# Sixteen-head attentions on one core: one tile of keys weighed at a time, and the small products made over two steps

## What is computed

```python
# L1, once: causal, 16 heads of 8 features
qkv = einsum('btc,cd->btd', x, w_qkv) + b_qkv
scores = einsum('bhqd,bhkd->bhqk', q, k) * scale
attn = softmax(where(causal, scores, min), axis=-1)
out = einsum('bhqk,bhkd->bhqd', attn, v)
return einsum('btc,cd->btd', out, w_out) + b_out

# L3, twice: M = 2 attentions of 16 heads each, no mask
q  = einsum('btd,mdhk->mbhtk', n1, mha_wq) + mha_bq
kk = einsum('btd,mdhk->mbhtk', n1, mha_wk) + mha_bk
v  = einsum('btd,mdhk->mbhtk', n1, mha_wv) + mha_bv
attn = softmax(einsum('mbhtk,mbhsk->mbhts', q, kk) / sqrt(KD), axis=-1)
ctx = einsum('mbhts,mbhsk->mbthk', attn, v)
x = x + einsum('mbtd,bm->btd', einsum('mbthk,mhkd->mbtd', ctx, mha_wo) + mha_bo, mha_probs)
```

## Time and profile before

| | |
|---|---|
| median of three runs | 2229.13 us |
| the profiled execution | 2221.16 us, span 2219.4 us |
| TensorE (PE) busy | 1751.5 us, 79% of the span |
| weight loads (PEld) busy | 902.8 us, 41% |
| VectorE (DVE) busy | 1308.6 us, 59% |
| ScalarE (ACT) busy | 1137.3 us, 51% |
| POOL busy | 609.9 us, 27% |
| mean granted clock of TensorE | 0.897 of full speed |

### The profile page before, as it was taken

How to read it: one execution, slowest core, us unless ns; L and a number is a source line. 1 busy time by engine, 2 the same in 40 slices (tenths; PEclk the granted TensorE clock), 3 DMA queues, 4 the chain that set the end, 5 groups by cost and what they waited for, 6 DMA issues and landing times.

```text
span 2219.4 us, 36295 instructions
## 1 busy us (share of the span) xinstructions
PE 1751.5 (79%) x13656; PEld 902.8 (41%) x13656; DVE 1308.6 (59%) x2653; ACT 1137.3 (51%) x2394; POOL 609.9 (27%) x759
## 2 busy tenths in 40 slices
PE   5997889687798879879387855868899576898875
PEld 1554255432355435543144322324444252344434
DVE  4773477343676358635577458446777444777744
ACT  3655256441465436545246645545776544467761
POOL 2541155200453025410255104223221021332202
PEclk8998999897899899989669977977999887799987
DMA  4000000000000000000152000034442021544303
GB/s 165 16 16 6 5 16 16 6 0 1 10 16 16 1 10 16 16 1 0 36 100 48 1 0 0 0 60 82 87 86 54 1 76 28 102 82 84 70 2 95
DMA packets 55269, 79.18 MB, mean 36 GB/s; under 512 B 6004, under 2 KB 38996, under 8 KB 54584
## 3 DMA queue, kind: packets, MB, share of 16 engines
q1 hardware_dynamic: 52536, 68.47, 14.2%
q0 software_dynamic: 2560, 8.39, 1.4%
HBM read 50.59 MB, written 16.88 MB: 30 GB/s over the span
## 4 chain that ended last, share of the span: by engine, by line
PE 58%; DVE 17%; ACT 13%; issue 7%; POOL 2%; DMA 2%; SPq 0%; DVEq 0%; POOLq 0%; ACTq 0%
PE ps L195 53%; ACT arena L540 4%; DVE arena L1204 3%; PE ps L459 2%; DVE arena L596 2%; ACT arena L267 2%; ACT arena L269 2%; DVE arena L639 1%; DVE arena L1202 1%; PE ps L1087 1%; ACT arena L263 1%; DVE arena L968 1%; DVE arena L970 1%; DMA arena<-scratch 1%; DVE arena L966 1%
## 5 line engine op out<-in xcount | busy, mean ns | idle before, releaser
L195 PE MATMUL ps<-arena 32*64 32x128 f32 (+10 forms) x10192 | 754.7, 319 | 177.6 <-DVE arena L1204 47.0
L195 PEld LDWEIGHTS ps<-arena 128*18 128x18 f32 (+6 forms) x10192 | 412.7, 129 | 513.8 <-DVE arena L1204 136.2
L1204 DVE TENSOR_REDUCE arena<-ps 128x2 f32<-128x512 f32 x512 | 325.7, 686 | 150.8 <-PE ps L195 148.1
L195 PE MATMUL ps<-arena,w_L0f 128*128 128x512 f32 (+3 forms) x800 | 348.4, 568 | 39.0 <-ACT arena L287 14.5
L1183 ACT ACTIVATE arena<-ps 128x1024 f32<-128x1024 f32 (+1 forms) x320 | 312.4, 981 | 97.0 <-PE ps L195 95.0
L540 ACT ACTIVATE arena<-ps,arena 128x128 f32<-128x128 f32 x512 | 226.2, 460 | 139.5 <-DVE arena L641 139.5
L195 PE MATMUL ps<-arena,const 128*128 128x512 f32 (+1 forms) x528 | 178.2, 639 | 60.4 <-DVE arena L1632 21.9
L195 PEld LDWEIGHTS ps<-arena,w_L0f 128*128 128x128 f32 (+2 forms) x800 | 147.5, 202 | 171.8 <-issue 125.6
L711 POOL TENSOR_TENSOR arena<-arena 128x512 f32<-128x512 f32 x128 | 132.2, 1039 | 240.1 <-DVE arena L613 240.1
L596 DVE TENSOR_TENSOR arena<-ps,arena 128x1024 f32<-128x1024 f32 x128 | 153.3, 1206 | 18.6 <-PE ps L195 18.6
L703 POOL TENSOR_TENSOR arena<-arena 128x512 f32<-128x512 f32 x64 | 81.2, 1269 | 218.8 <-DVE arena L596 216.0
(11 more groups left out here) (223 smaller groups left out, 2155.3 us busy)
## 6 DMA issues: line engine op xcount, KB each, us to landing
scratch<-arena SPq DMA_DIRECT2D x40, 384.0 KB, 2.8
arena<-scratch SPq DMA_DIRECT2D x80, 192.0 KB
arena<-scratch SPq DMA_DIRECT2D x80, 128.0 KB
arena<-arena SPq DMA_DIRECT2D x64, 128.0 KB, 2.3
arena<-scratch SPq DMA_DIRECT2D x80, 88.0 KB
w_L0f<-in_L0f SPq DMA_DIRECT2D x2, 1557.0 KB, 12.1
arena<-arena SPq DMA_DIRECT2D x80, 12.0 KB
const<-in_const SPq DMA_DIRECT2D x1, 1276.0 KB, 7.5
```

The lines of the kernel that those rows point to most:

```text
L195: return self.nc.tensor.matmul(o, lhsT, rhs, start=start, stop=stop, skip_group_check=True)
L1204: o = V.tensor_reduce(mx, ps[:, i % 2, :].rearrange("p (t s) -> p t s", t=2), AXX, ALU.max)
```

## The change

The quad is cut into its two tiles of keys: `quad_at` takes a number of tiles, and `weigh` makes one tile. The first tile stands at `LAG + 5`, the second two steps later, in both forms of the attention. In L3 the first tile stays where the quad was (steps 2, 6, 10, 14) and the second moves two steps back (0, 4, 8, 12 of the walk that follows); in L1 the second stays where the quad was (0, 4, 8, 12) and the first moves two steps ahead (14, 2, 6, 10). `weighed` is raised by the second.

The products of bank 7 move and are spread over steps: q at step 1 and k at step 2 (both at 0 before), turned maxima at 4 (3), the turn's halves at 6 and 7 (5), the values' halves at 9 and 10 (7), contexts at 12 (9), the outputs of two members at 14 and 15 (11; L1, with one member, only waits at 14). ScalarE's and VectorE's parts move with the last half of each. POOL's and SP's programs stay as they are.

```diff
--- before.py
+++ after.py
@@ -1026,7 +1026,7 @@
...
-        for s in range(-2 * HEADS, HEADS * (self.units + 2) + 12):
+        for s in range(-2 * HEADS, HEADS * (self.units + 2) + 16):
             yield s, s // HEADS, s % HEADS
@@ -1034,9 +1034,9 @@
...
-    def quad_at(self, s):
-
-        s -= self.LAG + (7 if self.causal else 5)
+    def quad_at(self, s, tiles=0):
+
+        s -= self.LAG + 5 + 2 * tiles
         w = s // 4
@@ -1053,22 +1053,21 @@
...
         for s, k, i in self.steps():
-            if s == 1 - 2 * HEADS:
+            if s == 3 - 2 * HEADS:
                 self.route_tensor(eng)
             u = k + 2
-            if i == 0 and self.is_unit(u):
+            if i == 1 and self.is_unit(u):
                 self.wait_ge(eng, self.biased, u)
...
                     self.wait_prepared(eng)
-                ms, bs = self.member(u), self.tokens(u)
-                for y, name in enumerate(("wq", "wk")):
-                    o = mm(ps[:, 7, y * SEQ:(y + 1) * SEQ], k_.wp(self.group, name)[:, ms], self.h[:, bs])
-                o.then_inc(self.projected.sem, 1)
+                self.project(u, 0)
+            if i == 2 and self.is_unit(u):
+                self.project(u, 1).then_inc(self.projected.sem, 1)
             u = k - 1
-            if i == 3 and self.is_unit(u):
+            if i == 4 and self.is_unit(u):
                 self.wait_ge(eng, self.mx_split, u + 1)
@@ -1077,32 +1076,33 @@
...
             u = k - 3
-            if i == 5 and self.is_unit(u):
+            if i == 6 and self.is_unit(u):
                 self.wait_ge(eng, self.raw_copied, u + 1)
...
                 self.wait_out(eng, k - 4)
-                for t in range(2):
-                    for c in range(2):
-                        o = T.transpose(ps[:, 7, (2 * t + c) * P:(2 * t + c + 1) * P], self.raw[:, c * SEQ + t * P:c * SEQ + (t + 1) * P], k_.K("ident"))
-                o.then_inc(self.turned.sem, 1)
-            if i == 7 and self.is_unit(k):
+                self.turn(0)
+            if i == 7 and self.is_unit(u):
+                self.turn(1).then_inc(self.turned.sem, 1)
+            if i == 9 and self.is_unit(k):
                 self.wait_ge(eng, self.biased, min(k + 3, U))
...
                 self.wait_ge(eng, self.scaled, k - 2)
-                ms, b0 = self.member(k), k // self.members * SEQ
-                for t in range(2):
-                    o = mm(ps[:, 7, t * P:(t + 1) * P], self.h[:, b0 + t * P:b0 + (t + 1) * P], k_.wp(self.group, "wv")[:, ms])
-                o.then_inc(self.valued.sem, 1)
-            if i == 9 and self.is_unit(u):
+                self.value(k, 0)
+            if i == 10 and self.is_unit(k):
+                self.value(k, 1).then_inc(self.valued.sem, 1)
+            if i == 12 and self.is_unit(u):
                 self.wait_ge(eng, self.scaled, u + 1)
...
                 o.then_inc(self.turned_again.sem, 1)
-            if i == 11 and self.ends_batch(u):
+            if i == 14 and self.ends_batch(u):
                 self.wait_ge(eng, self.ctx_copied, u + 1)
-                self.out_tensor(u // self.members)
+                if self.members > 1:
+                    self.out_tensor(u // self.members, 0)
+            if i == 15 and self.ends_batch(u):
+                self.out_tensor(u // self.members, self.members - 1).then_inc(self.summed.sem, 1)
             if self.is_unit(k):
@@ -1136,35 +1136,57 @@
...
                     self.wait_ge(eng, self.raw_copied, u)
-                c, j = x // 2, x % 2
-                for t, (st, cnt, at) in enumerate(((0, SEQ, 0), (SEQ - self.n1, self.n1, SEQ))):
-                    for f in range(4):
-                        h = 4 * x + f
-                        v = self.va[u % 3][:, t * HEADS + h, (KD + 1) * (1 - j):(KD + 1) * (3 - j)]
-                        o = mm(ps[32 * f:32 * f + 2 * (KD + 1), 6, c * SEQ + st:c * SEQ + st + cnt], v,
-                               self.pt[(2 * w + f // 2) % 4][:, f % 2, at:at + cnt], start=j == 0 and t == 0, stop=j == 1 and t == 1)
-                o.then_inc(self.weighed.sem, 1)
+                self.weigh(w, 0)
+            w = self.quad_at(s, 1)
+            if w is not None:
+                self.weigh(w, 1).then_inc(self.weighed.sem, 1)
+
+    def project(self, u, y):
+
+        return self.k.mm(self.k.ps[:, 7, y * SEQ:(y + 1) * SEQ], self.k.wp(self.group, ("wq", "wk")[y])[:, self.member(u)], self.h[:, self.tokens(u)])
+
+    def turn(self, t):
+
+        for c in range(2):
+            o = self.k.nc.tensor.transpose(self.k.ps[:, 7, (2 * t + c) * P:(2 * t + c + 1) * P], self.raw[:, c * SEQ + t * P:c * SEQ + (t + 1) * P], self.k.K("ident"))
+        return o
+
+    def value(self, u, t):
+
+        b0 = u // self.members * SEQ + t * P
+        return self.k.mm(self.k.ps[:, 7, t * P:(t + 1) * P], self.h[:, b0:b0 + P], self.k.wp(self.group, "wv")[:, self.member(u)])
+
+    def weigh(self, w, t):
+
+        u, x = w // self.QUADS, w % self.QUADS
+        c, j = x // 2, x % 2
+        st, cnt, at = (SEQ - self.n1, self.n1, SEQ) if t else (0, SEQ, 0)
+        for f in range(4):
+            v = self.va[u % 3][:, t * HEADS + 4 * x + f, (KD + 1) * (1 - j):(KD + 1) * (3 - j)]
+            o = self.k.mm(self.k.ps[32 * f:32 * f + 2 * (KD + 1), 6, c * SEQ + st:c * SEQ + st + cnt], v,
+                          self.pt[(2 * w + f // 2) % 4][:, f % 2, at:at + cnt], start=j == 0 and t == 0, stop=j == 1 and t == 1)
+        return o
...
         for s, k, i in self.steps():
-            if s == 1 - 2 * HEADS:
+            if s == 3 - 2 * HEADS:
                 self.route_scalar(eng)
             u = k + 2
-            if i == 0 and self.is_unit(u):
+            if i == 2 and self.is_unit(u):
                 self.wait_ge(eng, self.projected, u + 1)
...
             u = k - 1
-            if i == 3 and self.is_unit(u):
+            if i == 4 and self.is_unit(u):
                 self.wait_ge(eng, self.mx_turned, u + 1)
...
                 S.activation(self.mx_rows[u % 2], ps[0:PARTS * HEADS, 7, 0:SEQ], ACT.Copy).then_inc(self.mx_copied.sem, 1)
-            if i == 7 and self.is_unit(k):
+            if i == 10 and self.is_unit(k):
                 self.wait_ge(eng, self.valued, k + 1)
@@ -1181,7 +1203,7 @@
...
                 S.activation(self.pt[g % 4][:, :, 0:both], ps[:, bank:bank + 2, 0:both], ACT.Exp, scale=self.scale).then_inc(self.exped.sem, 1)
-            w = self.quad_at(s)
+            w = self.quad_at(s, 1)
             if w is not None and w % self.QUADS == self.QUADS - 1:
@@ -1351,8 +1373,8 @@
...
-    def out_tensor(self, b):
-        self.k.mm(self.k.ps[:, 7, 0:SEQ], self.k.wp("L1a", "wo"), self.ctxT[b % 2]).then_inc(self.summed.sem, 1)
+    def out_tensor(self, b, j):
+        return self.k.mm(self.k.ps[:, 7, 0:SEQ], self.k.wp("L1a", "wo"), self.ctxT[b % 2])
@@ -1851,11 +1873,9 @@
...
-    def out_tensor(self, b):
+    def out_tensor(self, b, j):
         k = self.k
-        for j in range(M_EXPERTS):
-            m = k.mm(k.ps[:, 7, 0:SEQ], k.wp("L3m", "wo")[:, j * P:(j + 1) * P], self.ctxT[j], start=j == 0, stop=j == M_EXPERTS - 1)
-        m.then_inc(self.summed.sem, 1)
+        return k.mm(k.ps[:, 7, 0:SEQ], k.wp("L3m", "wo")[:, j * P:(j + 1) * P], self.ctxT[j], start=j == 0, stop=j == M_EXPERTS - 1)
```

## The result

The changed kernel took 2308.66 us (median of four runs, 2302.65 to 2316.35), beside 2230.05 us for the kernel before on the same chip: a ratio of 1.034 (95% interval 1.031 to 1.038), slower. 2219.1 was forecast, with 2240 as the upper end.

A forecast was written before the change was run, and what follows sets the result against it. TensorE bounds the kernel, waiting about 10% of the time on uneven steps. L3 batches -13.5, drain -4, fill -2 and L1 +9 give -10.5, rounded to -10: 2219.1 us from the median, range 2196 to 2240.

The forecast's parts named there:

- Removed and added work: All three stages: same matmuls, evictions and DMAs; the quad's split costs 0, its bound below 0.1 us a half.
- The new waits: L3 unit: turned maxima 0.39, values 0.78, contexts 0.29, bank 6 0.31 us; with output, VectorE's addition 0.44.
- the old waits: L3 unit: TensorE's 2.3 us of waits for VectorE would vanish.
- Rival B: New waits eat the old: L3 units unchanged, end effects -5, L1 loses 9, about 2233 us; chance 0.18.
- Rival A: Levelling wins more: L3 waits less than laid out, L1 at +5, -32 in all, about 2199 us; chance 0.22.
- Drain and fill: Ends of both L3 stages: drain -2 us a stage, fill -1 us a stage.
- 13.5 batches: Both L3 stages: batches of two units going from 30.0 to 29.0 us, -13.5 us.
- SP's queue: L3: copies of the maxima start one step later; if their cover is gone, some 0.3 us a unit.
- +9 us, with ends 0 and +24: L1's total: early half quads wait about 3.3 us for POOL's selects, making the stage 9 us slower.
- +1 each for k = 4 and 5: L1 units k = 4 and 5: a clock drop after the 3.3 us wait adds 1 us each.
- six like pauses of 1.4 us: Kernel before: only one of six such pauses threw the clock back, taken against rival C's rule.
- Rival C: L1, k = 2 to 5: each 3.3 us pause halves the clock, +7 a unit; +14 in all, about 2243 us; chance 0.15.

The follow-up runs named there:

- 1: Kernel before with only the quads halved, at the changed kernel's steps, products where they were: 2214.5 us, ratio 0.996.
- experiment 3: Changed kernel with only the halves of L1's quads two steps later: 2284.6 us, ratio 1.029.
- 7: Against the changed kernel: L1 with late halves, moved products uncut; L3 with half quads and only values or turn cut: 2257.6 us, ratio 1.013.
- 5: Kernel before with late half quads in L1; L3 with half quads and projections spread (first stage) or the other products (second): 2230.0 us, ratio 1.005.
- 8: L1 of 7 with early halves; L3 with whole quads and moved uncut products, or half quads and cut projections: 2268.0 us, ratio 1.018.
- 10: L1 of 7 with the first projection made five times in two units; L3 half quads, output divided or turn at step 5: 2225.4 us, ratio 1.002.
- 6: Changed L1 with half the turn repeated six times in a pause; L3 half quads, products moved whole or cut near old steps: 2253.2 us, ratio 1.015.
- spread only: Changed kernel with whole quads at their old steps, products still spread, one wait added: 2340.4 us, ratio 1.055.

## Why the prediction was wrong

**"Removed and added work: none … I cost the split itself at 0; its bound is below 0.1 us a half."** This is the step that failed in L3. The same matmuls were issued, but TensorE needed 29.4 us a batch for them where 25.1 had been laid out. The durations were taken from rows in which kinds stand in long rows together; the change takes the switches from 33 to 61 a batch, and (29.4 - 25.3) / 28 is 0.15 us for each. That is a mean, fitted to these kernels and not a mechanism shown: the division of the quads cost 0.9 us of work a batch, of the values 0.7, of the output 0.5, of the projections 0.3, of the turn nothing, and moving whole products 1.3. Single distances show where the layout was short: 0.63 us for a projection (0.53 laid out), 0.39 to 0.42 for half of the values (0.31), 0.37 for half of the turn (0.30), 0.88 for scores with a half quad and the step to the next matmul (0.75). By these, a product's cost is its duration and something for the change of kind on both sides.

**The new waits.** Three came, near their sizes: 0.81 us for the values (0.78), 0.48 for the addition (0.44), 0.20 for bank 6 (0.31). Those of the turned maxima (0.39) and of the contexts (0.29) did not appear. The vanishing of the old waits was right too: in the two units above TensorE never waits for VectorE's reduction. Rival B had 4.7 us of old waits a batch replaced by as many new ones; in fact 2.6 remained, and B's units would have stood at 14.28 and 15.73. Work beyond any rival's made them 15.54 and 16.45. (Rival A's sum is 2 us off: -32 from the median of 2229.1 is 2197, not 2199; nothing hangs on it.)

**Drain and fill: -6 us.** The two stages grew by 25.6 us, and 13.5 batches at 2.0 make 27, which leaves 1 to 2 us of gain for them. From the last unit's turned maxima to the stage's end, nearly all drain, it is 22.4 and 21.6 us for 21.4 and 22.1 before; with half quads alone (1) it is 20.4 in both. So a gain of 1.0 and 1.7 us in the drain was there with half quads alone, and is gone with the spread.

**SP's queue: 0 to 0.3 us a unit.** No pair waits for the copies of the maxima in the changed L3, so 0 was right.

**L1, "+9 us, with ends 0 and +24".** It was +53. The wait was right in place and size, 2.85 us for 3.3 in the two units k = 4 and 5 (at most 1.67 in the two before them). The failed step is "+1 each for k = 4 and 5" for the clock. The clock was taken as a surcharge on a pause, paid in the steps behind it, and never as the state of a whole stage. (The reading under it was short as well: of the "six like pauses of 1.4 us" five are of 1.38 and one is of 1.64, ended at 1216.8, and the clock fell after two of the six, at 1153.6 and at 1218.5.) It came out at half for 168 of 212 us, and the seventh unit, which has no such wait at all, took 20.1 us where full clock gives 13.5. By these two figures a microsecond at half the clock costs 0.33 us (an estimate); the changed L1 has 111 of them more than the one before (168 for 57), which would be 36 of the 53 us. Rival C had the right place and sign, but priced four units at +7. As a sum of runs the 53 us are: 16 from the early halves, which wait for POOL's selects (experiment 3), 30 from the products' new steps (7 against 5), and 4 from their division (7) and 3 more, both within the spread of the unchanged stage (159 to 167 us in the kernels before, 4 and 9). The terms don't simply add: with undivided products early halves cost nothing (191.8 for 191.7 us, 8 against 7), and the early halves cost 18 alone and the spread 15. Of the 30, the same estimate gives 26 to the clock (134 us at half in 7, 56 in 5). The missing early rise is part of that: a dense stretch brought 10 us back, net of its own matmuls (10). The moved projections are another: POOL's splits start two steps later, and even late halves then wait up to 1.96 us (7). What in the new steps keeps the clock low stays open: no run takes the moved products apart in L1.

The Trainium skill tells of another kernel in this state ("TensorE: Matmul & The Clock Gate", A second HAM failure mode: psum-queue depth-cycling): TensorE idles often and briefly between groups of matmuls, and its clock swings between the levels. The changed L1 agrees in part, with four rises and four falls from 1177 us to its end; it also shows a stretch from 1208 to 1259 us that stays at half with TensorE shown 96% busy, of which no run here shows the cause.

## What to carry to other kernels

In this kernel TensorE's work was not the sum of its instructions' durations. So before cutting a piece in two to fill a wait, count how many changes of kind (tile shape, data type) the new order has, price them at what a trace of a mixed stretch shows (0.15 us here, as a mean), and cut only what stands before a wait, as the quads do. Try the whole piece at the new step first: in L3 that took 1.5 us of waits off a batch and put 1.3 of work on (6), and one step more or less brought a wait back (10). The same move in L1 cost 30 us, so try each stage by itself. And in a stage that starts at half the clock, ask what brings it up and whether the change spreads that out, since there a unit took 20.1 us for 13.5.

## What the hardware showed that was not expected

- TensorE's busy share says nothing of how much it does: 87.9 us busy of 100 with 682 matmuls at a clock of 0.59, 83.5 with 1039 at 0.92.
- The same unit takes 1.49 times as long at half the clock (20.11 and 13.52 us), with the other engines' busy times within 0.4 us of each other.
- Added matmuls can pay for themselves: eight repeated projections (sixteen matmuls) left a stage 10 us shorter (181.8 for 191.7), yet in another order of the same stage they changed nothing (195.9 for 196.1).
- In one stage a unit with output took 18.1 us at full clock, and 22.0 where the clock fell within it, with the same list of steps (spread only).
- An undivided move can raise TensorE's work by 1.3 us a batch (26.2 to 27.5) with only six more switches.
